# The causal mask multiplies of an attention stage moved from VectorE to GpSimd

## The chip, the cores and the metric

The kernel runs on the 8 cores of one Trainium2 chip. Each core takes one of the 8 batch entries of `x` (2048 tokens by 1024 features) through two layers, with no traffic between cores. The metric is the time of one execution on the device in microseconds, that of the slowest core. The engines are called as in the profile: PE (TensorE, matmul; PEld its weight load), DVE (VectorE), ACT (ScalarE), POOL (GpSimd), SP (SyncE, here for DMAs alone).

## The reference, cut to what matters

Layer 0 is a layer norm, causal attention with 16 heads of 64, beside it a feed-forward block whose operands are quantized to FP4 in blocks of 16, and a residual. Layer 1 (a gated scan and a mixture of 8 experts) is not touched by the change.

```python
xn = _layernorm(x)
# attention
q, k, v = (einsum('bse,hde->bshd', xn, W) + b for W, b in ...)
mask = triu(full((s, s), -inf), k=1)
attn = softmax((einsum('bqhd,bkhd->bhqk', q, k) + mask) * inv_scale)
s = einsum('bhqk,bkhd->bqhd', attn, v)
# feed-forward, with w_gate and w_up quantized before use
def fp4_quant_dequant(x):            # blocks of 16 along the last dim
    scale = maximum(max(abs(xb)) / 6, 1e-12)
    q = _GRID[searchsorted(_MID, abs(xb / scale))] * sign(xb) * scale
g = silu(fp4_linear(silu(gate) * up, w_down))
x = x + s * g
```

## The kernel before

One function per stage writes out the order of every engine (`narrative`); it is played five times, once for each engine, so each engine's queue holds its own instructions in the order of the code. Waits between engines are semaphores: `p.ved` counts VectorE's completions, `p.sed` ScalarE's, `p.ted` TensorE's, `p.pod` GpSimd's. A barrier stands between the four stages: attention (A), FP4 feed-forward (B), scan (C), experts (D).

The attention (`make_l0_attn`) first normalizes and transposes x and makes q, k and v. Then come four query tiles (`qt`, 0 to 3) of 512 tokens, in each of them eight head pairs (`hp`), and for each pair `nkc` = 4, 8, 12 or 16 key steps (`kc`) of 128 keys. A key step is: two score matmuls (L385, L389), two exponentials on ACT into `expA` and `expB` (L400, L401), and two matmuls with v (the AV matmuls, L427, L429) that add into PSUM. PE's order is scores of a step, then AV of the same step, then scores of the next one. The causal mask is needed in the last four key steps of a pair alone, on the diagonal: there `expA` and `expB` (128x512, bf16, double-buffered) are multiplied in place by a 0/1 mask (L409, L412), and L427 waits for that. So tile 0 has four masked steps to a pair and no unmasked ones, and tiles 1, 2 and 3 have 4, 8 and 12 unmasked steps ahead of the four.

Behind each pair `emit_wq_unit` puts one unit of other work into the queues, two in tiles 1 and 2: 128 rows of the feed-forward weights `wgu` are quantized ahead of stage B. There are 44 units: 8 in tile 0, 16 in tile 1, 16 in tile 2 and 4 in tile 3. A unit is, in this order: a load issued by POOL (L343) into one of two `wrowA`; eleven operations on DVE (L526 to L547, here called the head), whose last one signals POOL; two multiplies on POOL (L553, L556), whose last one is waited for by the store; and a store issued by POOL (L357). A unit's head also waits for the unit before it, since `q1A` and `q2A` exist once.

At the end of a query tile PE transposes the results and DVE copies and scales them (the tail copies, L473 to L491), behind the heads in its queue; the next tile's first scores and first AV matmul wait for these.

Of the kernel before, what the change touches and what calls it, by code (L numbers as in the profile page):

```python
# [120 lines left out]
def make_l0_attn(nc, dram, pq, pfx="a_"):  # L121
# [25 lines left out]
    expA = nc.alloc_sbuf_tensor_at("expA", [128, 2 * 512], BF16, offset=_wa + 32768)  # L147
    expB = nc.alloc_sbuf_tensor_at("expB", [128, 2 * 512], BF16, offset=_wa + 34816)
# [25 lines left out]
    def narrative(p):  # L174
# [157 lines left out]
        def emit_wq_unit():  # L332
            u = wq_state["u"]
            if wgu_h is None or u >= len(WQ_UNITS):
                return
            wq_state["u"] = u + 1
            sl_ = u % 2
            if u < 2:
                p.gp.wait_ge(p.ted.h, te_v_done)
            else:  # L340
                p.gp.wait_ge(p.ved.h, wq_state["head"][u - 2])
            srow = WQ_UNITS[u]
            p.gp.dma_start(out=wrowA[sl_][:],  # L343
                           in_=wgu_h.ap()[srow:srow + 128, :]) \
                .then_inc(p.gw0.h, 16)
            gv = p.gw0.bump(16)
            st_ = [p.gw1, p.gw2][sl_]
            p.ve.wait_ge(p.gw0.h, gv)
            if u >= 2:
                p.ve.wait_ge(st_.h, st_.v)  # L350
            vh, pt = _emit_quant(p, qbfA[sl_][:], wrowA[sl_][:], q1A, q2A,
                                 blkA, D, boff=0,
                                 wait_pod=wq_state["pt"].get(u - 1))
            wq_state["head"][u] = vh
            wq_state["pt"][u] = pt
            p.gp.wait_ge(p.pod.h, pt)
            p.gp.dma_start(out=wqp_h.ap()[u * 128:(u + 1) * 128, :],  # L357
                           in_=qbfA[sl_][:]).then_inc(st_.h, 16)
            st_.bump(16)
# [8 lines left out]
        for qt in range(4):  # L368
            nkc = (qt + 1) * 4
            for hp in range(NP):  # L370
                se_exp = {}
                te_av = {}
                for kc in range(nkc):
                    sa_ = pq[kc % 2]
                    sb_ = pq[2 + kc % 2]
                    if kc == 0:
                        p.te.wait_ge(p.ved.h, ve_vall)
                        p.te.wait_ge(p.sed.h, se_qkv[-1])
                        if se_exp_prev is not None:
                            p.te.wait_ge(p.sed.h, se_exp_prev)  # L380
                        if hp == 0 and ve_tail02 is not None:
                            p.te.wait_ge(p.ved.h, ve_tail02)
                    if kc >= 2:
                        p.te.wait_ge(p.sed.h, se_exp[kc - 2])
                    p.te.matmul(sa_[:],  # L385
                                kT[0:64, hp * S + kc * 128: hp * S + kc * 128 + 128],
                                qT[0:64, hp * S + qt * 512: hp * S + (qt + 1) * 512],
                                start=True, stop=True, tile_position=(0, 0))
                    p.te.matmul(sb_[:],  # L389
                                kT[64:128, hp * S + kc * 128: hp * S + kc * 128 + 128],  # L390
                                qT[64:128, hp * S + qt * 512: hp * S + (qt + 1) * 512],
                                start=True, stop=True, tile_position=(64, 0)) \
                        .then_inc(p.ted.h, 1)
                    te_s = p.ted.bump()

                    esl = kc % 2
                    p.se.wait_ge(p.ted.h, te_s)
                    if kc >= 2:
                        p.se.wait_ge(p.ted.h, te_av[kc - 2])
                    p.se.activation(expA[:, esl * 512:(esl + 1) * 512], sa_[:], AF.Exp)  # L400
                    p.se.activation(expB[:, esl * 512:(esl + 1) * 512], sb_[:], AF.Exp) \  # L401
                        .then_inc(p.sed.h, 1)
                    se_exp[kc] = p.sed.bump()

                    masked = kc >= nkc - 4
                    if masked:
                        mi = kc - (nkc - 4)
                        p.ve.wait_ge(p.sed.h, se_exp[kc])
                        p.ve.tensor_tensor(expA[:, esl * 512:(esl + 1) * 512],  # L409
                                           expA[:, esl * 512:(esl + 1) * 512],  # L410
                                           masks[:, mi * 512:(mi + 1) * 512], ALU.mult)
                        p.ve.tensor_tensor(expB[:, esl * 512:(esl + 1) * 512],  # L412
                                           expB[:, esl * 512:(esl + 1) * 512],
                                           masks[:, mi * 512:(mi + 1) * 512], ALU.mult) \
                            .then_inc(p.ved.h, 1)
                        ve_mask = p.ved.bump()
                        p.te.wait_ge(p.ved.h, ve_mask)
                    else:
                        p.te.wait_ge(p.sed.h, se_exp[kc])
                    if kc == 0 and se_stq_prev is not None:  # L420
                        p.te.wait_ge(p.sed.h, se_stq_prev)
                    if kc == 0 and hp == 0 and ve_tail13 is not None:
                        p.te.wait_ge(p.ved.h, ve_tail13)
                    headA, headB = 2 * hp, 2 * hp + 1
                    vA = vsb[:, kc * H * 65 + headA * 65: kc * H * 65 + headA * 65 + 65]
                    vB = vsb[:, kc * H * 65 + headB * 65: kc * H * 65 + headB * 65 + 65]
                    p.te.matmul(pq[4][0:65, :], vA, expA[:, esl * 512:(esl + 1) * 512],  # L427
                                start=(kc == 0), stop=(kc == nkc - 1))
                    p.te.matmul(pq[5][0:65, :], vB, expB[:, esl * 512:(esl + 1) * 512],  # L429
                                start=(kc == 0), stop=(kc == nkc - 1)) \  # L430
                        .then_inc(p.ted.h, 1)
                    te_av[kc] = p.ted.bump()

                te_fin = te_av[nkc - 1]
                se_exp_prev = se_exp[nkc - 1]
                p.se.wait_ge(p.ted.h, te_fin)
                if hp == 0 and qt >= 1:
                    p.se.wait_ge(p.ted.h, te_str)
                cs = hp * 512
                p.se.activation(sTqe[:, cs:cs + 512], pq[4][0:65, :], AF.Identity)  # L440
                p.se.activation(sTqo[:, cs:cs + 512], pq[5][0:65, :], AF.Identity) \
                    .then_inc(p.sed.h, 1)
                se_stq_prev = p.sed.bump()
                emit_wq_unit()
                if qt in (1, 2):
                    emit_wq_unit()
# [1386 lines left out]
```

## Time and profile before

| | |
|---|---|
| median of 3 timed runs | 5980.12 us (5978.77 to 5981.72) |
| the profiled execution's own time | 6034.22 us |
| span of its slowest core (core 5) | 6032.7 us |
| spans of the 8 cores | 5949.1 to 6032.7 us |
| mean granted TensorE clock, cores 0 to 3 and 4 to 7 | 0.766, 0.758 |
| busy, share of the span | PE 59%, PEld 25%, DVE 35%, ACT 21%, POOL 11% |
| query tiles 0 to 3 on core 5, from | 318.3, 491.4, 828.8, 1207.0 us |
| the attention's key steps end, and stage B's first load starts | 1656, 1676 us |

All rows are from the slowest core of that one execution, with times from the span's start. "Busy" leaves out waits. A row of the timeline is one instruction; in brackets stand the idle time of its engine just before it and what ended it. The granted clock is TensorE's, where 1.00 is 2.4 GHz and 0.50 is 1.2 GHz.

### The profile page before, as it was taken

What the parts mean: (1) busy time and instruction counts of PE and PEld (TensorE: products, weight loads), DVE (VectorE), ACT (ScalarE), POOL (GpSimd) and SP (SyncE); (2) the same over time, 40 slices, a digit from 0 to 9 for tenths busy, and PEclk for the clock granted to TensorE, in tenths of its full rate; (3) what the DMA queues carried; (4) which work ended last, traced back from release to release, by engine and by line L of the source; (5) the groups of instructions that cost most, each with busy time, mean ns of one, the idle gap of its engine ahead of it and who ended that gap; (6) DMA issues with size and microseconds to landing.
All of it is one profiled execution on the core that took longest, in us unless ns stands there. A gap on an engine that the chain in (4) does not pass through costs nothing.

```text
span 6032.7 us, 45811 instructions; the slowest of 8 cores (5949.1 to 6032.7 us)
## 1 busy us (share of the span) xinstructions
PE 3543.4 (59%) x15560; PEld 1495.4 (25%) x15560; DVE 2096.9 (35%) x3269; ACT 1251.5 (21%) x2020; POOL 679.7 (11%) x475
## 2 busy tenths in 40 slices
PE   1933334444400666620551566329999999999993
PEld 0401000010000333310220222114444444444441
DVE  2154545531055577765323112231122122122123
ACT  1222213323311222200013111031121211211211
POOL 0012222210022233323100000000000000000000
PEclk9955555555555788865775988758899999999996
DMA  4001111100010100001252211540302303303304
GB/s 102 1 30 46 37 46 37 37 30 12 0 46 24 35 15 15 15 29 37 81 150 91 21 15 28 171 91 1 56 14 43 56 8 49 56 2 55 56 1 160
DMA packets 139218, 271.18 MB, mean 45 GB/s; under 512 B 41424, under 2 KB 74704, under 8 KB 137968
## 3 DMA queue, kind: packets, MB, share of 16 engines
q0 software_dynamic: 99840, 127.73, 12.0%
q1 hardware_dynamic: 36848, 132.13, 6.5%
q10 hardware_dynamic: 2304, 8.39, 0.4%
q8 instruction: 131, 2.15, 0.1%
q14 instruction: 95, 0.78, 0.0%
HBM read 299.33 MB, written 53.48 MB: 58 GB/s over the span
## 4 chain that ended last, share of the span: by engine, by line
PE 51%; DVE 18%; ACT 10%; DMA 7%; issue 5%; POOL 5%; DVEq 3%; ACTq 0%; SPq 0%; POOLq 0%
PE pq L1590 15%; PE pq L1562 15%; PE pq L1217 4%; PE pq L427 3%; ACT a_expA L400 3%; PE pq L385 2%; ACT a_expB L401 2%; PE pq L429 2%; PE pq L279 2%; POOL b_q L553 2%; POOL b_hb L556 1%; PE pq L874 1%; DVE b_q L534 1%; DVE b_q L544 1%; DVE b_blk L526 1%
## 5 line engine op out<-in xcount | busy, mean ns | idle before, releaser
L1562 PE MATMUL pq<-d_tT,d_w1e 128*128 128x512 bf16 x4096 | 921.3, 389 | 34.5 <-ACT d_hTh L1572 34.5
L1590 PE MATMUL pq<-d_w2e,d_hTh 128*128 128x512 bf16 x4096 | 915.5, 387 | 33.7 <-ACT d_hTh L1572 33.7
L1606 DVE SCALAR_TENSOR_TENSOR d_acc<-pq,d_comb,d_acc 128x512 f32<-128x512 f32 x256 | 192.3, 751 | 1473.0 <-PE pq L1590 1473.0
L427 PE MATMUL pq<-a_expA,a_vsb 128*65 128x512 bf16 x320 | 194.4, 608 | 744.6 <-DVE a_expB L412 461.1
L1572 ACT ACTIVATE d_hTh<-pq,d_b1s 128x512 bf16<-128x512 f32 x512 | 351.6, 687 | 1266.0 <-PE pq L1562 1266.0
L1562 PEld LDWEIGHTS pq<-d_tT,d_w1e 128*128 128x128 bf16 x4096 | 407.4, 100 | 544.6 <-issue 128.8
L1590 PEld LDWEIGHTS pq<-d_w2e,d_hTh 128*128 128x128 bf16 x4096 | 404.7, 99 | 544.4 <-issue 134.0
L400 ACT ACTIVATE a_expA<-pq 128x512 bf16<-128x512 f32 x320 | 190.9, 596 | 889.1 <-PE pq L389 889.1
L1217 PE MATMUL pq<-c_xn2T,c_wsl 128*128 128x512 bf16 x1024 | 266.1, 407 | 162.3 <-ACT c_ga L1227 81.6
L409 DVE TENSOR_TENSOR a_expA<-a_expA,a_masks_s 128x512 bf16<-128x512 bf16 x128 | 63.8, 498 | 612.1 <-ACT a_expB L401 612.1
L427 PEld LDWEIGHTS pq<-a_expA,a_vsb 128*65 128x65 bf16 x320 | 41.8, 131 | 897.0 <-issue 897.0
L553 POOL TENSOR_TENSOR b_q<-b_q,b_blk 128x1024 f32<-128x1024 f32 (+2 forms) x96 | 160.8, 1675 | 898.2 <-DVE b_q L547 858.9
L874 PE MATMUL pq<-b_wgTs,b_xqT 128*128 128x512 bf16 (+1 forms) x768 | 202.3, 416 | 13.7 <-ACT b_wuTs L856 13.7
L429 PE MATMUL pq<-a_expB,a_vsb 128*65 128x512 bf16 x320 | 202.5, 633 | 0.0
L1609 DVE SCALAR_TENSOR_TENSOR d_acc<-d_b2b,d_comb,d_acc 128x512 f32<-128x512 f32 x256 | 192.3, 751 | 19.4 <-issue 0.4
L966 PE MATMUL pq<-b_ident_s,b_hb 128*128 128x128 bf16 x176 | 22.6, 306 | 299.8 <-POOL b_hb L556 299.8
L385 PE MATMUL pq<-a_qT,a_kT 64*128 64x512 bf16 x320 | 193.0, 603 | 4.3 <-DVE a_s0c L491 3.3
L389 PE MATMUL pq<-a_qT,a_kT 64*128 64x512 bf16 x320 | 193.6, 605 | 0.0
L1523 POOL DMA_DIRECT2D d_w1e<-w1T x32 | 28.3, 885 | 1440.4 <-PE pq L1562 1395.5
L401 ACT ACTIVATE a_expB<-pq 128x512 bf16<-128x512 f32 x320 | 189.3, 592 | 0.0
L553 POOL TENSOR_TENSOR a_q2A<-a_q2A,a_blkA 128x1024 f32<-128x1024 f32 x44 | 85.4, 1941 | 873.3 <-DVE a_q2A L547 873.3
L724 PE MATMUL pq<-b_ident_s,b_qbf 128*128 128x128 bf16 x128 | 16.2, 307 | 280.6 <-POOL b_qbf L556 280.6
(218 smaller groups left out, 4186.4 us busy)
## 6 DMA issues: line engine op xcount, KB each, us to landing
d_w1e<-w1T POOLq DMA_DIRECT2D x32, 1024.0 KB, 9.4
d_w2e<-w2T POOLq DMA_DIRECT2D x8, 4096.0 KB, 28.4
a_wrowA<-wgu POOLq DMA_DIRECT2D x44, 512.0 KB, 4.2
b_xt<-x SPq DMA_DIRECT2D x32, 512.0 KB, 4.6
wq_pre<-a_qbfA POOLq DMA_DIRECT2D x44, 256.0 KB, 2.4
b_wdr<-wd SPq DMA_DIRECT2D x8, 1408.0 KB, 6.1
a_xt<-x SPq DMA_DIRECT2D x16, 512.0 KB, 3.7
s<-a_s0c SPq DMA_DIRECT2D x16, 512.0 KB, 3.0
```

The costliest lines, as they stand in the source:

```text
L385: p.te.matmul(sa_[:], kT[0:64, hp * S + kc * 128: hp * S + kc * 128 + 128], qT[0:64, hp * S + qt * 512: hp * S + (qt + 1) * 512], start=Tr ...
L389: p.te.matmul(sb_[:], kT[64:128, hp * S + kc * 128: hp * S + kc * 128 + 128], qT[64:128, hp * S + qt * 512: hp * S + (qt + 1) * 512], star ...
L400: p.se.activation(expA[:, esl * 512:(esl + 1) * 512], sa_[:], AF.Exp)
L401: p.se.activation(expB[:, esl * 512:(esl + 1) * 512], sb_[:], AF.Exp) \
L427: p.te.matmul(pq[4][0:65, :], vA, expA[:, esl * 512:(esl + 1) * 512], start=(kc == 0), stop=(kc == nkc - 1))
L429: p.te.matmul(pq[5][0:65, :], vB, expB[:, esl * 512:(esl + 1) * 512], start=(kc == 0), stop=(kc == nkc - 1)) \
L553: p.gp.tensor_tensor(r3(t2), r3(t2), b3(hs[:]), ALU.mult) \
L874: p.te.matmul(gb[:, 0:hw], xqT[:, j * S + tc * 128: j * S + (tc + 1) * 128], wgTs[:, j * 512: j * 512 + hw], start=(j == 0), stop=(j == ND ...
L1217: inst = p.te.matmul(bank[:], wsl[sl][:, (w * ND + j) * 128:(w * ND + j + 1) * 128], xn2T[:, j * S + ch * 512: j * S + (ch + 1) * 512], st ...
L1562: inst = p.te.matmul(bank[:], w1e[:, j * MOE_H + hc * 128: j * MOE_H + (hc + 1) * 128], tT[:, j * S + hf * 512: j * S + (hf + 1) * 512], s ...
L1572: p.se.activation(hTh[:, hc * 512:(hc + 1) * 512], bank[:], AF.Gelu, bias=b1s[:, e * 16 + hc: e * 16 + hc + 1]) \
L1590: inst = p.te.matmul(bank[:], hTh[:, j * 512 + tr * 128: j * 512 + (tr + 1) * 128], w2e[:, j * D + dh * 512: j * D + (dh + 1) * 512], star ...
```

## The change

The two mask multiplies of a masked key step, and the wait for the exponentials ahead of them, are taken from VectorE's queue and put at the same place of the code into GpSimd's. The second multiply signals `pod` in place of `ved`, and the AV matmuls wait for that.

```diff
                     if masked:
                         mi = kc - (nkc - 4)
-                        p.ve.wait_ge(p.sed.h, se_exp[kc])
-                        p.ve.tensor_tensor(expA[:, esl * 512:(esl + 1) * 512],
+                        p.gp.wait_ge(p.sed.h, se_exp[kc])
+                        p.gp.tensor_tensor(expA[:, esl * 512:(esl + 1) * 512],
                                            expA[:, esl * 512:(esl + 1) * 512],
                                            masks[:, mi * 512:(mi + 1) * 512], ALU.mult)
-                        p.ve.tensor_tensor(expB[:, esl * 512:(esl + 1) * 512],
+                        p.gp.tensor_tensor(expB[:, esl * 512:(esl + 1) * 512],
                                            expB[:, esl * 512:(esl + 1) * 512],
                                            masks[:, mi * 512:(mi + 1) * 512], ALU.mult) \
-                            .then_inc(p.ved.h, 1)
-                        ve_mask = p.ved.bump()
-                        p.te.wait_ge(p.ved.h, ve_mask)
+                            .then_inc(p.pod.h, 1)
+                        pod_mask = p.pod.bump()
+                        p.te.wait_ge(p.pod.h, pod_mask)
```

POOL's queue in tile 0 before, from its first unit to the second one's load (`a_wrowA` is the loaded weight rows, `wq_pre` the stored result):

```order
L343 DMA a_wrowA_49<-wgu 128x1024
L553 TENSOR_TENSOR a_q2A<-a_q2A,a_blkA 128x1024
L556 TENSOR_TENSOR a_qbfA_53<-a_q1A,a_q2A 128x1024
L357 DMA wq_pre<-a_qbfA_53 128x1024
L343 DMA a_wrowA_50<-wgu 128x1024
```

The same place of POOL's queue now, from the last mask pair of the first head pair to the first mask pair of the second one:

```order
L409 TENSOR_TENSOR a_expA<-a_expA,a_masks_s 128x512
L412 TENSOR_TENSOR a_expB<-a_expB,a_masks_s 128x512
L343 DMA a_wrowA_49<-wgu 128x1024
L553 TENSOR_TENSOR a_q2A<-a_q2A,a_blkA 128x1024
L556 TENSOR_TENSOR a_qbfA_53<-a_q1A,a_q2A 128x1024
L357 DMA wq_pre<-a_qbfA_53 128x1024
L409 TENSOR_TENSOR a_expA<-a_expA,a_masks_s 128x512
L412 TENSOR_TENSOR a_expB<-a_expB,a_masks_s 128x512
```

Before, units followed each other on POOL; now four mask pairs of a head pair stand between one pair's units and the next one's (in tiles 1 and 2 two units stand between the masks of two head pairs).

DVE's queue between two head pairs of tile 0, as a piece of the difference: the end of a unit's head, the masks of the next head pair, and the start of the next head.

```order
 L546 TENSOR_SCALAR a_q1A<-a_q1A 128x1024
 L547 TENSOR_SCALAR a_q2A<-a_q2A 128x1024
-L409 TENSOR_TENSOR a_expA<-a_expA,a_masks_s 128x512
-L412 TENSOR_TENSOR a_expB<-a_expB,a_masks_s 128x512
-L409 TENSOR_TENSOR a_expA<-a_expA,a_masks_s 128x512
-L412 TENSOR_TENSOR a_expB<-a_expB,a_masks_s 128x512
-L409 TENSOR_TENSOR a_expA<-a_expA,a_masks_s 128x512
-L412 TENSOR_TENSOR a_expB<-a_expB,a_masks_s 128x512
-L409 TENSOR_TENSOR a_expA<-a_expA,a_masks_s 128x512
-L412 TENSOR_TENSOR a_expB<-a_expB,a_masks_s 128x512
 L526 TENSOR_REDUCE a_blkA<-a_wrowA_50 128x64
 L529 TENSOR_SCALAR a_blkA<-a_blkA 128x64
```

What is left on DVE there is one head after the other. The orders of PE, ACT and SP are the same as before.

## Rows read from the trace of the kernel before

**Rows 1.** Busy time in the attention stretch: length, engines, PEclk, DMA share, GB/s.
```profile
318.34:1674.00 1355.66, 534.93 (x1536) 122.59 (x1536) 537.15 (x837) 379.79 (x705) 240.64 (x176) 0.50 0.10 32
```

**Rows 2.** Waits, 290 to 1800 us: who waited for whom, total us, times, longest.
```profile
PE pq L427 <- DVE a_expB L412: 461.1, 128, 17.5
...
DVE a_blkA L526 <- DMA a_wrowA<-wgu: 164.8, 16, 12.0
```

**Rows 3.** Timeline, one head pair of tile 0: start us, us, instruction, [idle <-releaser].
```profile
379.04 1.21 DVE L526 TENSOR_REDUCE a_blkA<-a_wrowA 128x64 f32<-128x1024 f32 x1
...
387.46 0.42 DVE L409 TENSOR_TENSOR a_expA<-a_expA,a_masks_s 128x512 bf16<-128x512 bf16 x1
387.69 1.97 POOL L553 TENSOR_TENSOR a_q2A<-a_q2A,a_blkA 128x1024 f32<-128x1024 f32 x1 [16.21 <-DVE a_q2A L547]
387.79 2.15 DVE L412 TENSOR_TENSOR a_expB<-a_expB,a_masks_s 128x512 bf16<-128x512 bf16 x1
389.81 2.34 POOL L556 TENSOR_TENSOR a_qbfA<-a_q1A,a_q2A 128x1024 bf16<-128x1024 f32 x1
...
392.71 0.60 POOL L357 DMA_DIRECT2D wq_pre<-a_qbfA  x1 [0.56 <-POOL a_qbfA L556]
...
393.31 0.53 POOL L343 DMA_DIRECT2D a_wrowA<-wgu  x1
...
396.89 0.43 DVE L409 TENSOR_TENSOR a_expA<-a_expA,a_masks_s 128x512 bf16<-128x512 bf16 x1 [3.07 <-ACT a_expB L401]
...
397.80 0.61 PE L427 MATMUL pq<-a_expA,a_vsb 128*65 128x512 bf16 x1 [2.26 <-DVE a_expB L412]
...
400.71 0.43 DVE L409 TENSOR_TENSOR a_expA<-a_expA,a_masks_s 128x512 bf16<-128x512 bf16 x1 [3.06 <-ACT a_expB L401]
...
401.39 1.22 DVE L526 TENSOR_REDUCE a_blkA<-a_wrowA 128x64 f32<-128x1024 f32 x1
```

**Rows 4.** Groups by line, DVE: xcount, busy us, mean ns, idle before.
```profile
L412 DVE TENSOR_TENSOR a_expB<-a_expB,a_masks_s 128x512 bf16<-128x512 bf16 x128 | 92.5, 723 | 0.0
...
L409 DVE TENSOR_TENSOR a_expA<-a_expA,a_masks_s 128x512 bf16<-128x512 bf16 x128 | 63.8, 498 | 612.1 <-ACT a_expB L401 612.1
...
L544 DVE TENSOR_TENSOR a_q1A<-a_q1A,a_q2A 128x1024 f32<-128x1024 f32 x44 | 53.9, 1225 | 3.3
```

**Rows 5.** Timeline, two units between head pairs of tile 1.
```profile
538.82 1.22 DVE L526 TENSOR_REDUCE a_blkA<-a_wrowA 128x64 f32<-128x1024 f32 x1
...
553.04 0.53 POOL L343 DMA_DIRECT2D a_wrowA<-wgu  x1
...
567.53 0.42 DVE L409 TENSOR_TENSOR a_expA<-a_expA,a_masks_s 128x512 bf16<-128x512 bf16 x1
```

**Rows 6.** Groups by line and shape, POOL multiplies, largest first.
```profile
L553 POOL TENSOR_TENSOR b_q<-b_q,b_blk 128x1024 f32<-128x1024 f32 x72 | 139.0, 1930 | 787.3 <-DVE b_q L547 748.0 <-PE pq L879 39.3
L556 POOL TENSOR_TENSOR b_hb<-b_q 128x1024 bf16<-128x1024 f32 x56 | 131.1, 2341 | 8.3 <-POOL b_q L553 0.4
...
L556 POOL TENSOR_TENSOR b_hb<-b_q 128x768 bf16<-128x768 f32 x8 | 14.4, 1799 | 1.2
...
L556 POOL TENSOR_TENSOR b_hb<-b_q 128x256 bf16<-128x256 f32 x16 | 11.6, 723 | 2.3
L553 POOL TENSOR_TENSOR b_q<-b_q,b_blk 128x256 f32<-128x256 f32 x16 | 9.9, 620 | 53.1 <-DVE b_q L547 53.1
```

**Rows 7.** Source line L343, the weight load: time to landing.
```profile
DMA to landing us min/median/max: 3.7/4.2/6.5
```

**Rows 8.** Timeline from the end of tile 0 into tile 1.
```profile
505.86 0.60 POOL L357 DMA_DIRECT2D wq_pre<-a_qbfA  x1 [0.56 <-POOL a_qbfA L556]
...
522.52 0.60 ACT L400 ACTIVATE a_expA<-pq 128x512 bf16<-128x512 f32 x1 [1.88 <-PE pq L389]
...
525.48 0.60 ACT L400 ACTIVATE a_expA<-pq 128x512 bf16<-128x512 f32 x1 [1.88 <-PE pq L389]
...
526.67 0.43 DVE L409 TENSOR_TENSOR a_expA<-a_expA,a_masks_s 128x512 bf16<-128x512 bf16 x1 [11.89 <-ACT a_expB L401]
```


## The prediction

> **What bounds the kernel now.** I read the stretches first, to see which engine limits the stage that the change touches: the attention, 318 to 1674 us, where no engine is busy even half the time (PE 535 us, DVE 537 us of 1356) and the granted clock is 0.50, the 1.2 GHz level [rows 1]. Such a stage is bound by a chain, so I went on to the waits. PE stands 461.1 us before L427 for a mask, 128 times, 17.5 us at worst, and DVE 164.8 us for loads of the weight quantization, 16 times [rows 2]. The timeline of one head pair of query tile 0 shows the chain [rows 3]. DVE starts a unit's quantization head at 379.04, right behind the last mask of the pair; the next pair's first mask waits in the same queue until 387.46, so the head takes 8.42 us. POOL then begins the unit's second half at 387.69: two multiplies, a store, and the next load at 393.31. The mask begun 0.10 us after the POOL multiply takes 2.15 us in place of 0.42 [rows 3, 4]. From then on a step is mask, AV matmuls, next scores, exponentials, mask: 3.82 us (396.89 to 400.71), of which 0.91 us go from the start of the mask pair to the AV matmul that waited for it. The head pair repeats after 22.35 us (379.04 to 401.39). In tiles 1 and 2 two units stand between pairs, and the second one's load is issued only when POOL has finished the first: 28.71 us from the first head to the first mask (538.82 to 567.53), with that load at 553.04 [rows 5].
>
> **The change part by part.** It moves 256 multiplies of 128x512 from DVE to POOL. The units stay as they are; but POOL's queue is in program order too, and it now has the masks and the POOL parts of each unit in one line, as the listings of the change show. Four terms follow.
>
> *(a) The masks themselves.* The trace has no bf16 multiply on POOL, so I bound it. A full two-operand multiply there (L556) takes 2.341 us for 1024 columns, 1.799 for 768, 0.723 for 256: a line of 2.107 ns a column and 0.184 us fixed, so 1.26 us at 512 (an estimate). L553, one operand of which is a repeated block scale, takes 1.930 and 0.620 us for 1024 and 256 columns, so 1.06 at 512. If half the bytes cost like half the columns, the nearest row is 0.620 us (256 columns); if narrow types cost extra, 1.799 us (768 columns) [rows 6]. I take 1.26, since the output of L556 is bf16 already and both of its operands are full tensors; 0.62 and 1.80 are the ends. With 0.15 us until a waiter for POOL starts (387.69 + 1.97 to 389.81 [rows 3]) a pair takes 2 x 1.26 + 0.15 = 2.67 us, 1.76 more than 0.91. PE's order is scores, AV, scores, so nothing hides it: 128 x 1.76 = +225 us. The ends: 128 x (1.24 + 0.15 - 0.91) = +61, and 128 x (3.60 + 0.15 - 0.91) = +364.
>
> DVE multiplies f32 tensors of 1024 columns in 1.225 us (L544) and a bf16 mask in 0.42 [rows 4], where POOL's L556 needs 2.341 for 1024 columns [rows 6]. The Trainium skill ("GPSIMD Engine Reference", section "Performance versus the Vector engine") has f32 element-wise work on this engine at about twice DVE's time, 1.96 in its table; the trace agrees with 2.341/1.225 = 1.91. By that ratio on the bf16 mask it would be 0.82 us here, and the whole sum 6283 us (an estimate). I don't take it for bf16, where DVE's gain over its own f32 rate need not exist on POOL; no run here shows it yet.
>
> *(b) Stalls that go.* L412 is busy 92.5 us where 128 x 0.42 would be 53.8, L409 63.8 where 128 x 0.43 would be 55.0 [rows 4]: 48 us of masks held up by a POOL multiply. Now a mask and a unit's POOL half are on one queue and can't overlap: -48 us.
>
> *(c) Loads that lose their cover.* Before, POOL issues a unit's load while masks still run (393.31, for a head at 401.39). Now L343 stands behind the pair's last mask on POOL, and DVE has nothing to quantize until it lands. From the last mask: 0.56 us until POOL issues a DMA behind a multiply (the idle before L357 [rows 3]) and 4.2 us to land (3.7 to 6.5 [rows 7]), 4.8 us. It counts for the first unit of each pair of tiles 0, 1 and 2, 8 x 3 = 24 times; the eighth of a tile stands before the tile's tail copies, which follow the heads in DVE's queue. The second units of tiles 1 and 2 are exposed already (the 16 waits [rows 2]). The four units of tile 3 are hidden: an unmasked step takes 2.96 us (522.52 to 525.48 [rows 8]) and twelve of them 35.5, more than load, head and POOL's half together (4.8 + 8.42 + 5.85 = 19.1). So 24 x 4.8 = +115 us; ends 24 x 4.26 = +102 and 24 x 7.06 = +169.
>
> *(d) POOL's half before the first mask.* The head stays in front of the next pair's first mask, now by way of POOL, since the unit's second half waits for the head and the masks queue behind that half. DVE's mask could start at 387.46; POOL is through with multiplies and store at 393.31, 5.85 us later [rows 3]. This counts for pairs 1 to 7 of tiles 0, 1 and 2: 21 x 5.85 = +123 us. For a tile's first pair the store is issued at 505.86 and the first mask is due at 526.67 [rows 8]; the tail copies and unmasked steps hide it. Tile 2 has eight unmasked steps, 23.7 us, less than the 28.71 that two units take without (c) and (d), so it hides neither.
>
> Nothing else is late. DVE loses work that it had no time for in the chain, and gets no new waiter. SP's stores hang on the tail copies. The later stages start at a barrier and shift whole. The clock is at its low level already, and PE waits more than before.
>
> Sum: 225 - 48 + 115 + 123 = +415 us. The profiled execution took 6034.2 us with a span of 6032.7; the median of the timed runs is 5980.1, 54 below. All cores carry out the same attention, so I add the sum to the median: 6395 us, 6.9% more.
>
> **The rivals.**
> *R1, DVE's queue gets free and that is what counts.* An ordinary wait of PE for a mask is 2.26 us (397.80 [rows 3]); 128 of these are 289 of the 461.1 us, so all queueing and stalls on DVE together cost 172. If POOL took the masks ahead of its half of the unit, (c) and (d) would vanish and the 172 us go: 225 - 172 = +53, 6033 us. It decides for faster from the point where a pair costs less than 172/128 = 1.34 us more, a mask under 1.05 us; at 0.62 it is 61 - 172 = -111, 5869 us. For it: the head's 8.42 us before a mask are gone from DVE. Against it: POOL's order, row by row, with a wait at its head.
> In that case masks on POOL would run beside heads on DVE, as L412 ran beside L553 here: begun at 387.79, it ended at 389.94, after the POOL multiply (389.66). The Trainium skill ("SBUF — State Buffer", section "Who interferes with whom") says that a DVE instruction with two SBUF inputs and a GpSimd one that reads SBUF exclude each other; by that rule, with which the row agrees, R1 would give back part of its gain.
> *R2, POOL does bf16 at half the price.* Mask at 0.62: 61 - 48 + 115 + 123 = +251, 6231 us. For it: half the bytes. Against it: L556 writes bf16 and is no cheaper per column than L553, which writes f32.
> *R3, POOL is slow on bf16.* Mask at 1.80: 364 - 48 + 115 + 123 = +554, 6534 us. For it: L556 with its bf16 output is 0.41 us slower at 1024 columns than L553. Against it: L553's repeated operand explains that as well.
>
> **How the numbers follow.** Forecast 0.76, R2 0.11, R3 0.09, R1 0.04. By itself the forecast reaches from 6330 (mask 1.06, lower end of (c)) to 6470 (mask 1.45 and half of (c)'s upper end). The range goes part of the way to R2 and R3, a mask of 0.85 to 1.65 us: 6290 to 6495. A measurement of this kernel tells 0.2%, 12 us, from no change. Faster only by R1 with a cheap mask: 0.03; the same 0.01; slower 0.96.
>
> **What would show it.** (a) L409 and L412 on POOL near 1.26 us each, the masked step near 3.82 + 1.76 = 5.6 us. (b) No long mask. (c) DVE waiting at L526 for a load some 40 times in place of 16. (d) A pair's first mask right behind L357 on POOL. PE's waits for masks at L427 grow from 461 to some 860 us. Head pairs of tile 0 lie some 38 us apart in place of 22.35; those of tile 3 grow by four mask terms alone, 7.0 us. The forecast is wrong if a mask on POOL runs before the unit that stands ahead of it, if a mask takes under 0.85 us or over 1.65, or if a later stage changes its length.

## The result, and the profile after

Measured: 6368.58 us median against 5995.89 us for the kernel before in the same runs; ratio 1.0615, 95% interval 1.0563 to 1.0666: slower by 6.1%, where 6.9% (6395 us) was forecast. Some executions fall into a state in which the cores of one die show a lower clock; the ratios leave those out (the medians do not), and where a run here has no ratio, its attention stage is compared instead, which ran at the granted clock of 0.50 in every kernel.

The first view is the table of stretches of the changed kernel's attention (columns as in [rows 1]; slowest core, now core 4).

```profile
318.34:2031.00 1712.66, 535.57 (x1539) 122.72 (x1537) 395.27 (x581) 379.71 (x705) 528.13 (x432) 0.50 0.07 25
```

It is 1712.66 us long where it was 1355.66 in [rows 1]. PE and ACT are busy as long as before to 1 us, DVE 142 us less, POOL 287 us more, at the same clock. So the stretch holds 357 us more of waiting, where the ratio makes the whole execution some 368 us longer (0.0615 x 5980): the change of the time lies in this stage. For a comparison on one core, here is the evacuation at the end of every head pair (L440, ACT's copy of the results out of PSUM), first of before, then of after, both on core 4: count, shortest, median and longest ns, first and last start in us.

```profile
L440 ACT ACTIVATE a_sTqe<-pq x32: 593/593/593, 335.6 to 1652.1; 65x512 f32<-65x512 f32 x32
```

```profile
L440 ACT ACTIVATE a_sTqe<-pq x32: 592/592/593, 342.6 to 2013.3; 65x512 f32<-65x512 f32 x32
```

The last key step ends 361 us later (1652.1 to 2013.3). All lengths of the attention in the experiments below are read from this row, on core 4. How far apart the pairs of one tile lie is read from the same instruction's starts.

The waits of the same stretch (engine and line, waited for, total us, times, longest):

```profile
DVE a_blkA L526 <- DMA a_wrowA<-wgu: 1060.8, 44, 57.7
...
PE pq L427 <- POOL a_expB L412: 808.7, 128, 25.7
POOL a_q2A L553 <- DVE a_q2A L547: 538.0, 44, 13.3
```

PE's waits for masks have gone from 461.1 us [rows 2] to 808.7, and DVE waits for a load in front of every unit, 44 times in place of 16. Here is one head pair of tile 0, the place of [rows 3]:

```profile
359.92 1.16 POOL L409 TENSOR_TENSOR a_expA<-a_expA,a_masks_s 128x512 bf16<-128x512 bf16 x1
...
376.06 1.15 POOL L409 TENSOR_TENSOR a_expA<-a_expA,a_masks_s 128x512 bf16<-128x512 bf16 x1 [3.10 <-ACT a_expB L401]
377.17 1.15 POOL L412 TENSOR_TENSOR a_expB<-a_expB,a_masks_s 128x512 bf16<-128x512 bf16 x1
378.26 0.57 POOL L343 DMA_DIRECT2D a_wrowA<-wgu  x1
...
382.21 1.22 DVE L526 TENSOR_REDUCE a_blkA<-a_wrowA 128x64 f32<-128x1024 f32 x1 [28.03 <-DMA a_wrowA<-wgu]
...
390.03 0.69 DVE L547 TENSOR_SCALAR a_q2A<-a_q2A 128x1024 int32<-128x1024 int32 x1
390.88 1.92 POOL L553 TENSOR_TENSOR a_q2A<-a_q2A,a_blkA 128x1024 f32<-128x1024 f32 x1 [12.04 <-DVE a_q2A L547]
392.94 2.34 POOL L556 TENSOR_TENSOR a_qbfA<-a_q1A,a_q2A 128x1024 bf16<-128x1024 f32 x1
395.83 0.60 POOL L357 DMA_DIRECT2D wq_pre<-a_qbfA  x1 [0.56 <-POOL a_qbfA L556]
396.46 1.16 POOL L409 TENSOR_TENSOR a_expA<-a_expA,a_masks_s 128x512 bf16<-128x512 bf16 x1
397.56 1.16 POOL L412 TENSOR_TENSOR a_expB<-a_expB,a_masks_s 128x512 bf16<-128x512 bf16 x1
...
398.97 0.61 PE L427 MATMUL pq<-a_expA,a_vsb 128*65 128x512 bf16 x1 [18.93 <-POOL a_expB L412]
...
401.87 1.15 POOL L409 TENSOR_TENSOR a_expA<-a_expA,a_masks_s 128x512 bf16<-128x512 bf16 x1 [3.15 <-ACT a_expB L401]
```

The chain can be read off from top to bottom: last mask pair on POOL, load issued at 378.26 right behind it, head on DVE from 382.21, POOL's half from 390.88, store issued at 395.83, and only then the next pair's first mask at 396.46, for which PE has waited 18.93 us. The pair repeats after 36.5 us (359.92 to 396.46) in place of 22.35, and a masked step after 5.4 (396.46 to 401.87) in place of 3.82. The masks as a group, to be set beside [rows 6]:

```profile
L409 POOL TENSOR_TENSOR a_expA<-a_expA,a_masks_s 128x512 bf16<-128x512 bf16 x128 | 147.2, 1150 | 905.8 <-ACT a_expB L401 905.3
L412 POOL TENSOR_TENSOR a_expB<-a_expB,a_masks_s 128x512 bf16<-128x512 bf16 x128 | 147.0, 1149 | 0.0
```

### The profile page after: what moved, and what is told of

Same layout as the page of the kernel before. It is cut to its first block, busy times and chain, and to the rows that moved or that the text cites. A ratio compares the mean times of both kernels' runs of the same rounds, so it can differ in the third digit from the quotient of the medians.

```text
span 6402.3 us, 45555 instructions; the slowest of 8 cores (6324.1 to 6402.3 us)
## 1 busy us (share of the span) xinstructions
PE 3538.9 (55%) x15304; PEld 1498.6 (23%) x15560; DVE 1954.8 (31%) x3013; ACT 1251.2 (20%) x2020; POOL 967.3 (15%) x731
## 3 DMA queue, kind: packets, MB, share of 16 engines
q8 instruction: 131, 2.15, 0.1%
## 4 chain that ended last, share of the span: by engine, by line
PE 47%; DVE 17%; POOL 11%; ACT 9%; DMA 8%; issue 6%; DVEq 3%; ACTq 0%; POOLq 0%; SPq 0%
PE pq L1590 14%; PE pq L1562 14%; PE pq L1217 4%; DMA a_wrowA<-wgu 2%; POOL a_expB L412 2%; PE pq L427 2%; ACT a_expA L400 2%; POOL a_expA L409 2%; PE pq L279 2%; PE pq L385 2%; POOL b_q L553 2%; ACT a_expB L401 2%; PE pq L429 1%; PE pq L874 1%; POOL b_hb L556 1%
## 5 line engine op out<-in xcount | busy, mean ns | idle before, releaser
L427 PE MATMUL pq<-a_expA,a_vsb 128*65 128x512 bf16 x320 | 194.5, 608 | 1088.8 <-POOL a_expB L412 808.7
L526 DVE TENSOR_REDUCE a_blkA<-a_wrowA 128x64 f32<-128x1024 f32 x44 | 53.7, 1220 | 1060.8 <-DMA a_wrowA<-wgu 1060.8
L553 POOL TENSOR_TENSOR b_q<-b_q,b_blk 128x1024 f32<-128x1024 f32 (+2 forms) x96 | 160.8, 1675 | 900.2 <-DVE b_q L547 860.9
L409 POOL TENSOR_TENSOR a_expA<-a_expA,a_masks_s 128x512 bf16<-128x512 bf16 x128 | 147.2, 1150 | 905.8 <-ACT a_expB L401 905.3
L879 PE MATMUL pq<-b_wuTs,b_xqT 128*128 128x512 bf16 (+1 forms) x753 | 173.3, 372 | 0.8
```

The lines of the kernel that those rows point to most:

```text
L409: p.gp.tensor_tensor(expA[:, esl * 512:(esl + 1) * 512], expA[:, esl * 512:(esl + 1) * 512], masks[:, mi * 512:(mi + 1) * 512], ALU.mult)
L553: p.gp.tensor_tensor(r3(t2), r3(t2), b3(hs[:]), ALU.mult) \
```

## The experiments

The theory was the prediction's: masks dearer on POOL (a), no more stalls (b), loads without cover (c), POOL's half before the first mask (d), the last two from the order of POOL's queue. The main rival: only the slower multiply costs, and the order is indifferent.

**(a) alone, with nothing else in the queues.** Two kernels have all 44 units behind the attention, one with masks on DVE, one on POOL.

```diff
-                emit_wq_unit()
-                if qt in (1, 2):
-                    emit_wq_unit()
...
+        for _u in range(len(WQ_UNITS)):
+            emit_wq_unit()
```

Expected of the first: 

> Kernel before with masks on DVE, but all 44 units stand behind the attention in the queues, so nothing is queued with the masks. Own estimate 6500 us (44 bare units of 18 us come after the attention). To be compared with the next one in the attention's key steps alone.

Expected of the second: 

> The same with the masks on POOL. Queue theory (term a alone): key steps longer than in the run with DVE masks by 128 x 1.49 = 190 us, each mask 1.15 us as in the changed kernel. Rival 1, only POOL's slower multiply costs: longer by the whole 360 us. Rival 2, masks on POOL are slow because DVE's heads hold a port: masks get shorter than 1.15 us here.

The same row of the two, core 4:

```profile
L440 ACT ACTIVATE a_sTqe<-pq x32: 593/593/594, 334.6 to 1432.2; 65x512 f32<-65x512 f32 x32
```

```profile
L440 ACT ACTIVATE a_sTqe<-pq x32: 592/592/593, 341.5 to 1629.3; 65x512 f32<-65x512 f32 x32
```

1629.3 - 1432.2 = 197 us, near the 190 that were expected, and far from 360: the multiply's price is a good half of the loss and not all of it. With the two kernels of the change these two make a square: the units among the masks lengthen the attention by 1652.1 - 1432.2 = 220 us with masks on DVE, and by 2013.3 - 1629.3 = 384 us with masks on POOL. The 164 us between are what the new order costs, net of the stalls of (b) that went with it. The masks take 1.150 and 1.149 us there as in the changed kernel, so the heads on DVE are not what makes them slow:

```profile
L409 POOL TENSOR_TENSOR a_expA<-a_expA,a_masks_s 128x512 bf16<-128x512 bf16 x128 | 147.2, 1150 | 1329.7 <-ACT a_expB L401 1329.7
```

(The first one took 6608.5 us in its one timed run, for which 6500 had been estimated.)

**(c) alone.** One wait is added to the kernel before, whose masks are on DVE: the load of a pair's first unit waits for the pair's last mask.

```diff
+                p.gp.wait_ge(p.ved.h, ve_mask)
                 emit_wq_unit()
```

Expected: 

> Kernel before, masks on DVE, with one wait more: POOL issues the load of a pair's first unit only when the pair's last mask is done. Term c by itself: 24 loads of about 4 us (issue to head) exposed in tiles 0 to 2, the attention some 95 to 100 us longer than before. Rival, loads are covered by something else: 0.

```profile
L440 ACT ACTIVATE a_sTqe<-pq x32: 592/592/593, 334.3 to 1746.5; 65x512 f32<-65x512 f32 x32
```

1746.5 - 1652.1 = 94 us: the loads had been covered, as the theory has it. That it equals 24 x 3.95 = 95 us (issue at 378.26 to the head at 382.21 above) is in part chance, since the pairs did not all grow alike: by 4.7 us in tile 0, 4.4 in tile 1 and 2.8 in tile 2. In tile 0 the load here also waits 0.6 us for the mask's signal, which it does not in the changed kernel. In tile 2 another cost went: before, both of the first two masks of a head pair there were held up by POOL's multiplies, in six of the seven pairs that follow a unit, 3.8 us in the rows below (kernel before, core 4). With the later load the first mask starts right behind the head again, and only the second one is held up, 1.73 us as in [rows 3].

```profile
929.45 2.10 DVE L409 TENSOR_TENSOR a_expA<-a_expA,a_masks_s 128x512 bf16<-128x512 bf16 x1 [0.26 <-ACT a_expB L401]
931.47 2.56 DVE L412 TENSOR_TENSOR a_expB<-a_expB,a_masks_s 128x512 bf16<-128x512 bf16 x1
```

**(b) and (d) together.** Another wait in the kernel before: a pair's first mask, on DVE, waits for the last unit's POOL half.

```diff
                         p.ve.wait_ge(p.sed.h, se_exp[kc])
+                        lpt = wq_state["pt"].get(wq_state["u"] - 1)
+                        if mi == 0 and lpt:
+                            p.ve.wait_ge(p.pod.h, lpt)
```

Expected: 

> Kernel before, masks on DVE, with one wait more: a pair's first mask waits until POOL has finished the second half of the last unit (not its store). Terms b and d together: the first mask comes 4.8 us later (392.3 in place of 387.5 in tile 0), 21 times, and no mask is held up by a POOL multiply (1.73 us less each): 21 x 3.1 = 65 us longer. Rival, the stall of 1.73 us is most of what the POOL half costs in either order: about 0.

```profile
L443 ACT ACTIVATE a_sTqe<-pq x32: 593/593/594, 335.0 to 1705.3; 65x512 f32<-65x512 f32 x32
```

1705.3 - 1652.1 = 53 us (65 expected), and not 0. The pairs of tile 0 grew by 3.0 us as expected, those of tile 2 by 1.2 only, since the stalls that go there are the larger ones shown above, 3.8 us and not 1.73. What this kernel lacks of (d) is the store that POOL also issues before the mask (0.60 us behind 0.56 us of idle in [rows 3]; an estimate of some 1.1 us x 21 = 23 us). So the parts made singly come to 197 + 94 + 53 = 344 us, and to 367 with that estimate, against 361 measured. Each part stands in a kernel with waits of its own, so the sum shows that no large term is missing, and not each term to the microsecond.

**Undoing (c) in the changed kernel.** SP issues the loads, with a semaphore for each buffer, so that they don't stand behind the masks.

```diff
...
-            p.gp.dma_start(out=wrowA[sl_][:], ...).then_inc(p.gw0.h, 16)
+            ld_ = [p.sw0, p.sw1][sl_]
+            p.sy.dma_start(out=wrowA[sl_][:], ...).then_inc(ld_.h, 16)
...
```

Expected: 

> Changed kernel, but the unit's loads (L343) are issued by SP, so that they no longer stand behind the masks on POOL; the rest as changed. Queue theory (term c, and the exposed second loads too): DVE waits for none of the 40 loads of tiles 0 to 2, 40 x 3.9 us = 156 us less attention than the changed kernel, about 6210 us. Rival 1, only POOL's slower multiply costs: no change, 6370 us. Rival 2, loads are hidden anyway by POOL's half of the unit: under 30 us less.

```profile
L441 ACT ACTIVATE a_sTqe<-pq x32: 593/593/593, 341.7 to 1697.5; 65x512 f32<-65x512 f32 x32
```

The attention ends 316 us earlier than in the changed kernel (2013.3 - 1697.5), twice what was expected; ratio to the kernel before 1.0168 (1.0108 to 1.0229). The expectation had counted the loads and forgotten what the load sets off: with its data there, DVE starts the head beside the masks, and the head's 8.42 us leave the chain too. The timeline of tile 0 in this run shows it, and what it costs:

```profile
366.38 0.59 ACT L441 ACTIVATE a_sTqe<-pq 65x512 f32<-65x512 f32 x1 [3.67 <-PE pq L430]
...
367.14 2.34 POOL L557 TENSOR_TENSOR a_qbfA<-a_q1A,a_q2A 128x1024 bf16<-128x1024 f32 x1
...
369.58 1.22 DVE L527 TENSOR_REDUCE a_blkA<-a_wrowA 128x64 f32<-128x1024 f32 x1 [12.74 <-POOL a_qbfA L557]
...
370.63 1.16 POOL L410 TENSOR_TENSOR a_expA<-a_expA,a_masks_s 128x512 bf16<-128x512 bf16 x1
...
376.05 1.48 POOL L410 TENSOR_TENSOR a_expA<-a_expA,a_masks_s 128x512 bf16<-128x512 bf16 x1 [3.15 <-ACT a_expB L402]
376.60 1.48 DVE L542 TENSOR_SCALAR a_q2A<-a_q2A 128x1024 int32<-128x1024 int32 x1
377.50 1.59 POOL L413 TENSOR_TENSOR a_expB<-a_expB,a_masks_s 128x512 bf16<-128x512 bf16 x1
378.16 2.01 DVE L545 TENSOR_TENSOR a_q1A<-a_q1A,a_q2A 128x1024 f32<-128x1024 f32 x1
```

The head's first operation starts when the unit before it leaves POOL (369.58), and its later ones run beside the masks. Where they meet in the rows above, both are longer: masks of 1.48 and 1.59 us in place of 1.15, on DVE a one-operand pass of 1.48 in place of 0.69 (L542 of this kernel) and a multiply of 2.01 in place of 1.225 (its L545, L544 in [rows 4]). The pairs repeat after 24.7 us (366.38 and 391.08 at the evacuation, of which the first stands above), 36.5 in the changed kernel: 11.8 us less, near the 3.95 of the load and the 8.42 of the head together. 316 us is more than the 164 that the new order costs, because the head stood ahead of the next pair's masks in the kernel before too, and here it does not.

**Masks ahead of POOL's half (the order of rival R1).** A pair's first unit is loaded and begun at the pair's start, and its POOL half and store come behind the pair's masks. The second units of tiles 1 and 2 stay where they were.

```diff
             for hp in range(NP):
+                unit_a = emit_wq_head()
...
-                emit_wq_unit()
+                emit_wq_half(unit_a)
```

Expected: 

> Changed kernel, but a pair's first unit has its load and head at the pair's start and its POOL half behind the pair's masks, so masks no longer wait for that head (the prediction's R1 built on purpose). Queue theory (c and d): tile 0 pairs 36.5 to about 25 us, tiles 1 and 2 from 55 to about 43 and 46; some 280 us less, about 6090 us. If the two engines exclude each other, masks beside heads are longer than 1.15 us and the gain is smaller. Rival 1, only POOL's slower multiply costs: 6370 us.

```profile
L452 ACT ACTIVATE a_sTqe<-pq x32: 593/593/594, 341.2 to 1774.5; 65x512 f32<-65x512 f32 x32
```

239 us less than the changed kernel where some 280 were expected; the profiled execution took 6099.6 us. So another order of POOL's queue by itself gives back two thirds of the loss; this too takes a head off the chain that stood in it before. R1's own estimate of 6033 us was not reached. Here too masks beside heads are longer (up to 2.13 us, some 20 us over all of them), which takes part of the gain.

**The price of a bf16 multiply on POOL.** Each mask in two pieces of 256 columns.

```diff
+                        for c0 in (0, 256):
...
+                            ea = expA[:, esl * 512 + c0:esl * 512 + c0 + 256]
+                            p.gp.tensor_tensor(ea, ea, ms, ALU.mult)
...
```

Expected: 

> Changed kernel with each 128x512 mask multiply on POOL split in two of 128x256. Measures the price of a bf16 multiply by its width. By the slope of the f32 rows with a smaller fixed part (1.149 = 0.070 + 512 x 2.107 ns) a piece takes 0.61 us; by the fixed part of these rows with a smaller slope (0.184 + 512 x 1.885 ns) 0.67 us. Masked step 4 pieces, 0.2 to 0.4 us longer than 5.36 us; some 30 to 60 us over the changed kernel.

```profile
L412 POOL TENSOR_TENSOR a_expA<-a_expA,a_masks_s 128x256 bf16<-128x256 bf16 x256 | 165.3, 667 | 905.3 <-ACT a_expB L401 904.9
L416 POOL TENSOR_TENSOR a_expB<-a_expB,a_masks_s 128x256 bf16<-128x256 bf16 x256 | 165.0, 665 | 0.0
```

0.667 us for 256 columns and 1.150 for 512: 1.887 ns a column and 0.184 us fixed. The fixed part is that of the f32 rows to a few ns, the slope lies between L553 and L556 of [rows 6]. The attention ends 33 us later than in the changed kernel (2046.5 on core 4), in the 30 to 60 us expected.

**Units in the shade of unmasked steps.** If the order is what costs, units should stand where PE has unmasked steps to do. Two kernels have 0, 1, 2 and 3 (then 2) units at the start of each pair of tiles 0 to 3, and SP's loads; one has the masks on DVE, one on POOL.

```diff
             for hp in range(NP):
+                for _u in range((0, 1, 2, 3 if hp < 4 else 2)[qt]):
+                    emit_wq_unit()
...
-                emit_wq_unit()
-                if qt in (1, 2):
-                    emit_wq_unit()
```

Expected with masks on DVE: 

> Masks on DVE as before; units moved to the starts of pairs that have unmasked steps (0, 1, 2 and 3 or 2 a pair in tiles 0 to 3), loads issued by SP. Queue theory: no mask waits for a head, no head stands before the tail copies: about 225 us less than before, 5755 us. Rival 1, only the multiply's speed counts: 5980 us.

Expected with masks on POOL: 

> The same places of units and loads, masks on POOL. Queue theory: terms c and d are gone, term a stays: 190 us over the run with masks on DVE, about 5945 us, so near or under the kernel before. Rival 1, only POOL's slower multiply costs: 360 us over it, about 6115 us or more.

```profile
L443 ACT ACTIVATE a_sTqe<-pq x32: 592/592/593, 334.8 to 1448.2; 65x512 f32<-65x512 f32 x32
```

```profile
L443 ACT ACTIVATE a_sTqe<-pq x32: 592/592/593, 341.0 to 1662.3; 65x512 f32<-65x512 f32 x32
```

With masks on DVE the ratio to the kernel before is 0.9659 (0.9558 to 0.9760), the fastest version of all, 204 us less attention than before (some 225 us less time expected). Its pairs are as short as with no units among the masks at all (27.6 us in tile 1 both times, 41.0 before), so the units are hidden there. With masks on POOL it is 0.9999 (0.9962 to 1.0035): the better order pays for the dearer masks and no more. That is over 40 us above the 5945 us expected (its fastest run took 5988.39); between the two lie 1662.3 - 1448.2 = 214 us, 17 more than (a). The masks are nearly undisturbed there (1.16 us), and the pairs within a tile differ as in (a). The 17 us lie where one tile ends and the next begins: from a tile's last evacuation to the next tile's first, three times, the two kernels differ by 36 us, and by 18 in (a). Term (d) is not gone there. Around the first mask of tile 1 with masks on POOL:

```profile
516.51 1.22 DVE L526 TENSOR_REDUCE a_blkA<-a_wrowA 128x64 f32<-128x1024 f32 x1 [6.87 <-DMA a_wrowA<-wgu]
...
525.15 1.93 POOL L553 TENSOR_TENSOR a_q2A<-a_q2A,a_blkA 128x1024 f32<-128x1024 f32 x1 [32.13 <-DVE a_q2A L547]
...
530.73 1.17 POOL L412 TENSOR_TENSOR a_expA<-a_expA,a_masks_s 128x512 bf16<-128x512 bf16 x1
```

The head comes late, for its load is issued only at 510.12, behind the tile's stores on SP, and the first mask stands behind POOL's half, 5.6 us after that begins. With masks on DVE the first mask of this tile starts right behind the head (474.61).

## Why the prediction was right

*(a)* Forecast +225, measured +197. The step that was off is the size of a mask: 1.26 us from L556's line, 1.15 in the trace. The way there was sound (linear in columns, the fixed part right to a few ns), but L556 reads two f32 tensors and the masks read bf16, which took 1.887 ns a column and not 2.107. The bounds of 1.06 and 1.80 held, and the 0.62 of R2 did not come: half the input bytes took a tenth off the slope.

The rule that was weighed there, the Trainium skill's factor of about two to DVE ("GPSIMD Engine Reference", section "Performance versus the Vector engine"), would have given 0.82 us and 6283 us (an estimate); on bf16 the trace has 1.149/0.42 = 2.7. The measurement decides: the factor belongs to f32, where both rows stand here (1.91).

*(b)* Forecast -48. No mask is held up any more in the changed kernel (1.138 to 1.162 us all of them). The size was not measured by itself: in the run for (b) and (d) the two mask lines are busy 108 us, 48 less than the 156 of [rows 4], but that run has (d) too.

*(c)* Forecast +115; the run for it gave +94, and in the changed kernel's tile 0 a load takes 3.95 us in place of 4.8, 95 us for 24. The place and the count were right; the step that was off is the 0.56 us of idle, and with it the time to land. The 0.56 us of idle before a POOL DMA belong to a store that waits for the multiply just before it; a load behind a mask that it doesn't wait for is issued at once (378.26, where the mask ends at 378.32).

*(d)* Forecast +123. From the head's start to the next pair's first mask there were 8.42 us in [rows 3] and are 14.25 now (382.21 to 396.46): 5.83 more, x 21 = 122 us by this one pair.

By these, 197 - 48 + 94 + 122 = 365 us, 361 measured, 415 forecast: of the 54 us too much, 28 are the mask and 21 the load. The pairs bear it out tile by tile: (c), (d) and the stalls of (b) together were 8.0 us a pair in tiles 0 and 1 (14.2 more than before, less 6.1 of (a)), and 6.0 in tile 2. The prediction took the three tiles as alike, since tile 2's eight unmasked steps hide neither (c) nor (d); that held but for 0.26 us (the idle in the row of 929.45), while the larger stalls there stood in its 48 us of (b) and not in its picture of a pair. PE's waits came to 809 us for 860 forecast, tile 0's pairs to 36.5 for 38, and those of tile 3 grew by 6.1 us for 7.0. R1 fell with the order of POOL's queue; with R1's order 239 us came back. The later stages, from the last evacuation to the end of the span, differ by -10 to +19 us on the cores 0, 2, 4, 5 and 6, so no change of one sign shows there.

One step of the working was right for less than it says: the prediction priced (c) as 24 loads. In the changed kernel the load is also what ties the head to the masks, and undoing it gives back 316 us and not 94. The terms added up in going forward because each had its place in one chain; taken away alone, one of them breaks the chain.

## What to carry to other kernels

An engine with an in-order queue that issues DMAs, does the second half of other work and is now handed a step of the critical chain will put all three in one line: write down what stands ahead of each instruction before counting its own time. Work that fills gaps belongs where the critical chain has its long unmasked stretches, and its loads on a queue that does not wait in that chain; here the two together were worth 3.4% with masks left on DVE, though SP's queue too waited, at each tile's end. Price an operation on another engine from a row of the same input type, not only of the same output.

## What the runs showed of the hardware

A bf16 multiply of two full tensors on POOL took 0.184 us and 1.887 ns a column, against 0.184 us and 2.107 ns with f32 inputs, and 0.42 us for 512 columns on DVE. POOL and DVE multiplies that met could both be longer, not DVE's alone: 1.48 and 1.59 us for masks of 1.15, 2.01 for a DVE multiply of 1.225, and in the kernel before 2.15 for a mask of 0.42. The Trainium skill ("SBUF — State Buffer", section "Who interferes with whom") has a DVE instruction with two SBUF inputs and a GpSimd one that reads SBUF exclude each other; the traces agree for these multiplies. A DVE pass with one input was held up as well, 1.48 us in place of 0.69. A DMA on POOL's queue was issued with no idle time behind a multiply that it did not wait for (378.26), and 0.56 us after one that it did (395.83, and 24.4 us in 44 such waits).
